# Decoder with 16-wide heads: interleaved head stacks, one transfer for a group's shift rows, and key stacks written by DMA

## The reference, cut to what matters

```python
# self-attention: q, k, v of LayerNorm(x), 512 keys
w = jnp.einsum('bshd,bzhd->bhsz', q, k) / jnp.sqrt(16.) / jnp.sqrt(16.)
w = jax.nn.softmax(w, axis=-1)
vw = jnp.einsum('bhsz,bzhd->bshd', w, v)
# cross-attention: q of LayerNorm(x), k and v of ctx_1024 (1024 keys), rotary q and k
scores = jnp.einsum('bhqd,bhkd->bhqk', q, k) * 16 ** -0.5
out = jnp.einsum('bhqk,bhkd->bhqd', jax.nn.softmax(scores, axis=-1), v)
```

## Time and profile before

| | us |
|---|---|
| median of 3 runs | 2225.75 |
| the profiled execution, its own time | 2233.84 |
| its span in the trace | 2232.0 |
| PE busy | 1995.9 (89%) |
| DVE busy | 1722.2 (77%) |
| ACT busy | 1347.4 (60%) |
| POOL busy | 262.1 (12%) |

### The profile page before, as it was taken

The page is one execution under the profiler, slowest core; times in us unless marked ns, Lnnn a source line. Parts: engine busy times, 40 slices in busy tenths (PEclk is TensorE's granted clock), DMA queues, the critical chain, the costliest instruction groups (busy, mean ns, idle before and its releaser), DMA issues.

```text
span 2232.0 us, 42943 instructions
## 1 busy us (share of the span) xinstructions
PE 1995.9 (89%) x17926; PEld 1125.7 (50%) x17926; DVE 1722.2 (77%) x2660; ACT 1347.4 (60%) x2001; POOL 262.1 (12%) x279
## 2 busy tenths in 40 slices
PE   2899988988989997989899998798998999889888
PEld 1576653423756764232466666333255667533335
DVE  7788878695878877779587887868767878786956
ACT  3566656587356654848536664675944666565782
POOL 2000001350000000135000000103400000011520
PEclk9999999999999999999999999999999999989999
DMA  6176730020046780001006776001001767400100
GB/s 262 36 125 120 126 69 1 1 92 14 20 77 121 124 135 20 2 19 78 11 20 107 125 125 119 1 2 76 21 10 41 121 118 123 93 1 1 76 2 10
DMA packets 417313, 147.66 MB, mean 66 GB/s; under 512 B 404440, under 2 KB 412768, under 8 KB 416224
## 3 DMA queue, kind: packets, MB, share of 16 engines
q1 hardware_dynamic: 416544, 142.82, 31.3%
q0 software_dynamic: 576, 2.10, 0.3%
HBM read 41.86 MB, written 2.10 MB: 20 GB/s over the span
## 4 chain that ended last, share of the span: by engine, by line
PE 57%; DVE 25%; DMA 7%; ACT 6%; issue 3%; SPq 0%; POOL 0%; POOLq 0%; DVEq 0%; ACTq 0%
PE ps L622 10%; DVE nmx L1940 10%; PE ps L624 10%; PE ps L623 10%; DMA arena<-arena 7%; PE ps L970 5%; PE ps L784 3%; PE ps L1037 3%; PE ps L956 3%; DVE arena L1752 3%; PE ps L924 2%; PE ps L779 2%; PE ps L778 2%; DVE st L1584 1%; PE ps L980 1%
## 5 line engine op out<-in xcount | busy, mean ns | idle before, releaser
L1940 DVE TENSOR_REDUCE nmx<-ps 128x2 f32<-128x1024 f32 x384 | 446.0, 1218 | 32.4 <-PE ps L924 30.5
L1449 ACT ACTIVATE arena<-ps 128x512 f32<-128x512 f32 x768 | 405.4, 603 | 55.8 <-PE ps L956 51.1
L622 PE MATMUL ps<-arena 128*128 128x512 f16 (+1 forms) x800 | 275.7, 345 | 1.1 <-DVE arena L1674 0.5
L623 PE MATMUL ps<-arena 128*128 128x512 f16 (+1 forms) x800 | 275.1, 344 | 0.0
L624 PE MATMUL ps<-arena 128*128 128x512 f16 (+1 forms) x800 | 274.4, 343 | 0.0
L1739 DVE TENSOR_SCALAR_CACHE_REDUCE ps<-ps 128x1536 f32<-128x1536 f32 x128 | 225.8, 1764 | 48.9 <-PE ps L624 48.3
L970 PE MATMUL ps<-arena 128*17 128x256 f32 x3072 | 238.7, 387 | 0.0
L1752 DVE SCALAR_TENSOR_TENSOR arena<-arena,rs 128x1536 f16<-128x1536 f32 x128 | 231.6, 1810 | 4.2 <-ACT arena L1343 4.2
L1343 ACT ACTIVATE arena<-arena,rs 128x1536 f16<-128x1536 f32 x128 | 200.8, 1568 | 40.1 <-DVE rs L1745 40.1
L1336 ACT ACTIVATE arena<-ps,nm 128x1536 f32<-128x1536 f32 x128 | 197.0, 1539 | 12.5 <-DVE ps L1739 12.5
L594 POOL TENSOR_TENSOR rstd<-ve,col 128x2 f32<-128x2 f32 x40 | 29.3, 732 | 1346.1 <-DVE ve L1845 907.1
(11 more groups left out here) (280 smaller groups left out, 3854.8 us busy)
## 6 DMA issues: line engine op xcount, KB each, us to landing
arena<-in_experts SPq DMA_DIRECT2D x4, 3840.0 KB, 11.5
arena<-in_weights SPq DMA_DIRECT2D x8, 929.0 KB, 12.7
arena<-in_ctx SPq DMA_DIRECT2D x4, 1024.0 KB, 5.8
arena<-arena SPq DMA_TRANSPOSE x256, 3.7
arena<-in_ctx_t SPq DMA_DIRECT2D x4, 1024.0 KB, 4.8
arena<-in_ternary SPq DMA_DIRECT2D x2, 1024.0 KB, 5.9
y<-in_x POOLq DMA_DIRECT2D x4, 512.0 KB, 4.3
x<-in_x SPq DMA_DIRECT2D x4, 512.0 KB, 3.7
```

Source lines behind the costliest of these rows:

```text
L622: mm(out_, lh, rh, start=(k == 0), stop=False)
L623: mm(out_, lh, rl_, start=False, stop=False)
L1449: A(pr_[:, n % RING, :], ps[:, 4 + n % 3, :], ACT.Exp).then_inc(b_exp.sem, 1)
L1940: V.tensor_reduce(nmx[:, g_ % 2, ch, :, pp, i], ps[:, 2 * (z % 2):2 * (z % 2) + 2, :], AX.X, ALU.max, negate=True)\
```

## The change

The rows of a head are interleaved: dim d takes rows 4d, 4d+1, 4d+2 (copies 0, 1, 2) and row 4d+3 is a pad, of which rows 3 and 35 of each head carry the shift (key side -64 and +64, `HC = 3`). So copy r of a pair's 32 rows of halves is a DMA with a partition stride of 4. Pairs 0 and 1 of the keys are still made on PE and ACT. Pairs 2 to 7 come by three DMAs each from `dk` (32 KB each in self-attention, 64 KB in cross-attention): 18 DMAs in each attention, 36 in a batch. The pads of pairs 2 to 7 are written by one DMA for each batch, from a table that is made at the start of the launch and stored in DRAM. The query stacks are made as before.

The shift rows of a group go out in one DMA (4 rows of 2 KB from 32 partitions); for that the maxima are laid out twice (`nm32`, 32 columns), which in self-attention is an added instruction on DVE for each group, and in cross-attention the minimum over both key halves that was there already, now 32 columns wide.

```diff
+                sp.dma_start(ks[HC:P:4, 2:8, :], pad_d.unsqueeze(1).to_broadcast([P // 4, 6, NCTX])).then_inc(pad_in.sem, 16)
+                def stack_keys(m_, p_):
+                    c, jj = divmod(p_, 4)
+                    n = (S, NCTX)[m_]
+                    for copy, part in enumerate((0, 0, 1)):
+                        sp.dma_start(ks[copy:P:4, p_, 0:n], dk[part][32 * jj:32 * jj + 32, c, 0:n]).then_inc(ks_in[p_].sem, 16)
                 def shift_rows(mode, g_):
                     sp.wait_ge(sl_free.sem, sl_free.at(b, mode.slot0 + mode.z_shift[g_] + 1))
-                    for e in range(2):
-                        for part in range(2):
-                            r0 = 64 * e + HR + part
-                            sp.dma_start(qs[r0:r0 + 1, 2 * g_:2 * g_ + 2, :], sh[8 * e:8 * e + 8, g_ % 2, part, :])\
-                              .then_inc(sh_in.sem, 16)
-                for g_ in range(GROUPS):
+                    sp.dma_start(qs[HC:P:32, 2 * g_:2 * g_ + 2, :], sh[0:32, g_ % 2, :]).then_inc(sh_in.sem, 16)
+                sp.wait_ge(lq_lo.sem, lq_lo.at(b, 1))
+                for p_ in range(2, 4):
+                    stack_keys(0, p_)
+                sp.wait_ge(lq_lo.sem, lq_lo.at(b, 3))
+                for p_ in range(4, 6):
+                    stack_keys(0, p_)
+                shift_rows(MODES[0], 0)
+                for p_ in range(6, 8):
+                    stack_keys(0, p_)
+                for g_ in range(1, GROUPS):
                     shift_rows(MODES[0], g_)
+                sp.wait_ge(kp_first_lo.sem, kp_first_lo.at(b, 1))
+                sp.wait_ge(kp_lo.sem, kp_lo.at(b, 1))
+                for p_ in range(2, 4):
+                    stack_keys(1, p_)
                 shift_rows(MODES[1], 0)
-                for done, n in ((lv_mm, 6), (k_st, LH), (q_st, LH)):
+                sp.wait_ge(kp_lo.sem, kp_lo.at(b, 3))
+                for p_ in range(4, 8):
+                    stack_keys(1, p_)
+                for done, n in ((lv_mm, 6), (k_st, 4), (q_st, LH)):
                     sp.wait_ge(done.sem, done.at(b, n))
+                for p_ in range(2, 8):
+                    sp.wait_ge(ks_in[p_].sem, ks_in[p_].at(b, 96))
...
@@ score_slot (PE)
-                    n = LH // 2 * mode.m + 2 * g_ + pp + 1
-                    pe.wait_ge(k_st.sem, k_st.at(b, n))
-                    pe.wait_ge(q_st.sem, q_st.at(b, n))
+                    p_ = 2 * g_ + pp
+                    if p_ < 2:
+                        pe.wait_ge(k_st.sem, k_st.at(b, 2 * mode.m + p_ + 1))
+                    else:
+                        pe.wait_ge(ks_in[p_].sem, ks_in[p_].at(b, 48 * (mode.m + 1)))
...
@@ between_cross (PE; between_self alike)
                 elif a in CROSS_SELECT:
-                    select_k(b, 1, CROSS_SELECT.index(a) + 1)
+                    if a == CROSS_SELECT[0]:
+                        select_k(b, 1, 1)
                     select_q(b, 1, CROSS_SELECT.index(a) + 1)
...
@@ max_slot (DVE)
-                if mode.nch == 2 and (a + 1) % mode.per_group == 0:
+                if (a + 1) % mode.per_group == 0:
                     dve.wait_ge(sl_free.sem, sl_free.at(b, mode.slot0 + z + 1))
...
+                    if mode.nch == 2:
+                        last = TT(nm32[:, g_ % 2], by_ch[0], by_ch[1], ALU.min)
+                    else:
+                        last = TS_(nm32[:, g_ % 2], by_ch[0], 1.0, None, ALU.mult)
+                    last.then_inc(nm_done.sem, 1)
...
@@ start of the launch (DVE)
+            own.mark(V.tensor_reduce(sh_lo[:], pad[:, 0, :, HC], AX.X, ALU.add))
+            own.link(V.tensor_reduce(k_pad[:], pad[:, 1, :, HC], AX.X, ALU.add))
+            own.link(TT(k_pad[:], k_pad[:], sh_lo[:], ALU.subtract))
             own.link(TS_(k_pad[:], k_pad[:], 64.0, None, ALU.mult))
+            TS_(ks[:, 4, :], ks[:, 4, :], k_pad[:], None, ALU.mult).then_inc(pad_made.sem, 1)
+            second = ident[:].rearrange("p (e n) -> p e n", n=16)[:, 0:2, 8:16]
+            own.link(V.tensor_reduce(sh_lo[:], second, AX.XY, ALU.add))
+            own.link(TS_(sh_lo[:], sh_lo[:], 1.0 / 64.0, None, ALU.mult))
```

More of the change, by code:

```diff
@@ L32 @@
 LH, LD = 16, 16
-HR = 48
-SR = HR + 2
+HC = 3
 GROUPS = 4
@@ L253, in decoder @@
         assert lay.at == 98304
-        sh = lay.take([2, 2, P], F16)
+        sh = lay.take([2, P], F16)
         lay = Layout()
@@ L264, in decoder @@
         assert lay.at <= 53760
+        pad_d = nc.dram_tensor("pad_d", (P // 4, NCTX), F16, kind="Internal").ap()
         ps = c_.enter_context(nc.psum_tensor("ps", [P, 8, 512], F32))
@@ L283, in decoder @@
         sel_set = sig("sel_set")
-        sel_mm, k_st, q_st = sig("sel_mm", 32), sig("k_st", LH), sig("q_st", LH)
+        sel_mm, k_st, q_st = sig("sel_mm", 20), sig("k_st", 4), sig("q_st", LH)
+        pad_in, pad_made, pad_out = sig("pad_in", 16), sig("pad_made"), sig("pad_out")
+        ks_in = [None, None] + [sig(f"ks_in{p_}", 2 * 48) for p_ in range(2, 8)]
         var_ready, rstd_ready = sig("var_ready", 10), sig("rstd_ready", 10)
@@ L1482, in stacked_q @@
             def stacked_q(b, m_, p_):
-                act.wait_ge(sel_mm.sem, sel_mm.at(b, LH * m_ + 2 * p_ + 2))
+                act.wait_ge(sel_mm.sem, sel_mm.at(b, 10 * m_ + (2 * p_ + 2 if p_ < 2 else p_ + 3)))
                 A(qs[:, p_, :], ps[:, 5 + m_, :], ACT.Copy, scale=(LD ** -0.5, 1.0)[m_]).then_inc(q_st.sem, 1)
@@ L1941, in max_slot @@
                     .then_inc(sl_free.sem, 1)
-                if mode.nch == 2 and (a + 1) % mode.per_group == 0:
+                if (a + 1) % mode.per_group == 0:
                     dve.wait_ge(sl_free.sem, sl_free.at(b, mode.slot0 + z + 1))
-                    both_ch = nmx[:, g_ % 2].rearrange("p k e c i -> p k (e c i)")
-                    TT(both_ch[:, 0], both_ch[:, 0], both_ch[:, 1], ALU.min).then_inc(nm_done.sem, 1)
+                    by_ch = [nmx[:, g_ % 2, k].rearrange("p e c i -> p e (c i)").unsqueeze(2).to_broadcast([P, 2, 2, 2 * NT])
+                             for k in range(mode.nch)]
+                    if mode.nch == 2:
[3 more added lines that the diff above has]
+                    last.then_inc(nm_done.sem, 1)
             def shift_split(b, mode, g_):
@@ L1950, in shift_split @@
                 if n >= 2:
-                    dve.wait_ge(sh_in.sem, sh_in.at(b, 64 * (n - 1)))
+                    dve.wait_ge(sh_in.sem, sh_in.at(b, 16 * (n - 1)))
                 dve.wait_ge(sl_mm.sem, sl_mm.at(b, 2 * (mode.mm0 + z + 1)))
-                src = ps[0:16, 2 * (z % 2), 0:P]
-                own.link(TS_(sh[0:16, g_ % 2, 0, :], src, 1.0 / 64.0, None, ALU.mult))
-                STT(sh[0:16, g_ % 2, 1, :], src, 1.0 / 64.0, sh[0:16, g_ % 2, 0, :], ALU.mult, ALU.subtract)\
-                    .then_inc(sl_free.sem, 1)
+                src, dst = ps[0:32, 2 * (z % 2), 0:P], sh[0:32, g_ % 2, :]
+                own.link(TS_(dst, src, 1.0 / 64.0, None, ALU.mult))
+                STT(dst, src, sh_lo[0:32], dst, ALU.mult, ALU.subtract).then_inc(sl_free.sem, 1)
             def slots(b, mode, a0, a1):
@@ L2137, in _ @@
             own.mark(TS_(taps[:], col[:, COL["cw"]:COL["cw"] + 3 * NM], mw[:, 0:1], None, ALU.mult))
-            pad = ident[:].rearrange("p (e n) -> p e n", e=2)[:, :, HR:SR]
-            own.link(V.tensor_reduce(k_pad[:], pad, AX.XY, ALU.add))
+            pad = ident[:].rearrange("p (e h n) -> p h e n", e=2, h=2)
+            own.mark(V.tensor_reduce(sh_lo[:], pad[:, 0, :, HC], AX.X, ALU.add))
+            own.link(V.tensor_reduce(k_pad[:], pad[:, 1, :, HC], AX.X, ALU.add))
+            own.link(TT(k_pad[:], k_pad[:], sh_lo[:], ALU.subtract))
             own.link(TS_(k_pad[:], k_pad[:], 64.0, None, ALU.mult))
+            TS_(ks[:, 4, :], ks[:, 4, :], k_pad[:], None, ALU.mult).then_inc(pad_made.sem, 1)
+            second = ident[:].rearrange("p (e n) -> p e n", n=16)[:, 0:2, 8:16]
+            own.link(V.tensor_reduce(sh_lo[:], second, AX.XY, ALU.add))
+            own.link(TS_(sh_lo[:], sh_lo[:], 1.0 / 64.0, None, ALU.mult))
             dve.wait_ge(b2_hi.sem, 1)
```

45 lines of the change are left out of this document (29 added, 16 removed).

## The result

The changed kernel takes 2174.91 us (median of 4 runs, 2171.07 to 2176.4), the kernel before in the same comparison 2224.35 (2221.53 to 2230.8): ratio 0.976, 95% interval 0.974 to 0.978. The forecast was 2208 us, with a range from 2197 to 2221, so it gained 49 us where 18 were expected. The profiled executions are 2233.84 us (span 2232.0) and 2171.07 us (span 2169.3).

The account below looks back on a forecast made before the run. The prediction took PE (57% of the chain) and DVE (25%) as the bound, DVE setting the pace in mid cross-attention. Its terms summed to -17.7 us, taking the median from 2225.75 to 2208 us, range 2197 to 2221.

Parts of the forecast that it names:

- The change part by part: The prediction's list of terms, summed against the profiled execution of 2233.84 us; the difference to the median was carried over.
- selects of keys, cross-attention: Cross-attention's opening: without the key selects DVE no longer idles behind six slots; 4.0 us a batch, 16.0 us saved.
- one transfer for a group: Shift rows of both attentions: one DMA instead of four lands them 1.9 us earlier; 5.5 us saved, between 3 and 6.5.
- the experts' load: Cross-attention: the load, issued behind 12 stack DMAs, may delay group 1's shift rows; 2.0 us lost, between 0 and 8.
- the minimum beside POOL: Cross-attention: POOL starts later, so a DVE minimum takes 0.18 instead of 0.85 us; 1.4 us saved, at most 2.7.
- self-attention, selects and added copy: Self-attention: fewer key selects save 2.0 us, an added DVE copy for each group loses 3.6 us.
- start of the launch: Launch start: PE waits for extra small DVE instructions and the pads' product; 1.6 us lost, between 1 and 2.5.
- Rival C: Attention openings: PE, now waiting for DVE, drops to half clock; +70 us, 2296 us; chance 0.02.
- case D: Whole launch: the sum holds with its terms at their good ends; -27.4 us, 2198 us; chance 0.11.

Follow-up runs that it names:

- E2: The changed kernel with 224 unused bytes per partition ahead of the arena, as misplaced as before: 2202.25 us, ratio 0.987 to the kernel before.
- E1: The kernel before with six small tensors moved behind the arena, which then starts on a multiple of 512: 2200.84 us, ratio 0.987.
- E4: The changed kernel with key stacks of pairs 2 to 7 again made by PE and ACT: 2194.71 us, ratio 0.984 to the kernel before.
- E8: The changed kernel with a group's shift rows again sent by four transfers instead of one: 2201.40 us, ratio 0.987 to the kernel before.
- E11: The changed kernel with every key-stack transfer followed by another of its size: 2214.29 us, ratio 0.994 to the kernel before.
- E9: The changed kernel with 224 unused bytes ahead of the arena, but the transposes' source alone on a multiple of 256: 2176.78 us, ratio 0.977.

## Why the prediction was wrong

**The failed step** is the silent one in "The change part by part": only the two attentions and the start of the launch have terms, so the latent, windowed, routed and ternary stages were held unchanged because their instructions were. `nm32` and `sh_lo` moved the arena by 288 bytes, from 224 past a multiple of 256 to 0, and the transposes' source with it. The term was put at nothing; it is worth about 24 us (E2 against the changed kernel, 0.987 against 0.976 of 2225 us) to 30 us (E1), and it made the range miss. The mechanism is not in the prediction at all. It could have been asked for: the diff shows two tensors ahead of the arena, and TensorE's longest DMA waits were on these transposes.

The terms beside what was measured, in us over the launch:

| term | forecast | measured |
|---|---|---|
| latent and all other stages | 0 | -24 to -30 |
| selects of keys, cross-attention | -16.0 | -17.0 (E4, less the minima) |
| one transfer for a group | -5.5 | -6.1 (E1 to E4) |
| the experts' load | +2.0 | 0 |
| the minimum beside POOL | -1.4 | -1.9 |
| self-attention, selects and added copy | +1.6 | -0.1 (E1) to -0.7, in a scatter of some 5 |
| start of the launch | +1.6 | +1.3 |

**Selects of keys, cross-attention: right.** The forecast was 4.0 us a batch, at most 4.3; E4 gives 4.25. The opening of batch 0 gave 4.5, with 0.20 us behind slot 10 that the prediction had not listed. The query selects behind slots 13 to 16, of which I expected up to 0.45 us, left no idle time.

**The minimum: right, cause included.** The forecast had read from the earlier trace rows that the 0.85 us go with a working POOL, and took 1.4 us off. All traces bear this out.

**One transfer for a group: right when alone, wrong as a term to be added.** With the key stacks in the same queue it is worth 26 us (E8). In a row: from E1 the stacks by DMA alone give nothing (2201.4 against 2200.8), one transfer alone 6, both together 25. The sum came out near because the two were made together; that they depend on each other the prediction did not see.

**The experts' load: no loss.** The forecast was 0.5 us a batch, and 1.5 us with the long issue, which was the true one (0.62 us). There is no wait for group 1's rows. In batch 0 the load goes out at 454.4 and has landed at 466.5 by its slower part, 11.7 us after that part's issue, where I took 12.8; the rows are needed at 467.2. It is narrow, as E11 shows.

**Self-attention: not resolved.** E4, with the selects back on PE, takes 245.9 us, the changed kernel 246.8, E1 246.9. Neither the 0.5 us a batch of the selects nor the 0.9 of the copy can be told from the scatter.

**The start:** the wait before the first products is 32.4 us, 31.1 before: +1.3 for 1.6.

**Rival C** appears, small. Windows of the changed kernel's self-attention, batch 0 (columns as above):
```profile
356.00:360.00 4.00, 3.47 (x23) 1.16 (x21) 3.97 (x4) 2.55 (x6) 0.00 (x0) 1.00 0.13 36
360.00:362.00 2.00, 1.14 (x6) 0.42 (x6) 1.97 (x4) 1.96 (x5) 0.00 (x0) 0.82 0.00 0
362.00:368.00 6.00, 6.00 (x38) 0.98 (x37) 4.34 (x6) 3.06 (x6) 0.00 (x0) 0.50 0.02 4
```
After PE's less busy stretch (1.14 of 2.00 us) the granted clock is 0.50, the 1.2 GHz level, for 6 us, and VectorE waits 0.7 us twice. That batch's self-attention takes 62.9 us, the quickest 60.8. The kernel before had such a batch too (63.6 us; over 1993 to 2000 us PE is busy for 5.78 us with a clock of 0.87, over 2000 to 2010 the clock is 0.75). So the prediction's sentence that no window of before with so little work has a lower clock was read from three windows and is wrong for the whole trace. In cross-attention's opening, where I had placed C, the clock stays at 1.00:
```profile
432.00:446.00 14.00, 11.81 (x71) 4.53 (x70) 13.93 (x16) 5.38 (x9) 6.96 (x7) 1.00 0.00 1
```
**With the address held,** the change is worth 28.7 us by E2 (20 to 37 by its interval), both kernels 224 past a multiple of 256, and some 23 to 26 us by E1 against the changed kernel, both on a multiple. That would be 2197 to 2202 us, inside the range at its low edge, and near case D (2198) or the forecast's own low end (2202). What is above the 17.7 forecast and has a place is cross-attention: -25.0 us from E1 to the changed kernel for -20.9 forecast. Half of this difference of 4.1 us is the loss of 2.0 us at the experts' load that did not come. The few us between the two estimates are within the noise; the profiled execution of before was itself 8 us over its median.

## What to carry to other kernels

A new tensor of a few bytes moves every later one: before pricing a diff, ask what lies behind it and which DMA reads it; a DMA transpose whose source starts off a multiple of 256 bytes lost 0.9 to 1.3% of this kernel. Small transfers on a shared queue can't be priced one by one: what stands ahead of them decides, and slack is counted to the landing of the large transfer ahead, not to its issue. Here neither the stacks by DMA nor the single transfer gave a third of what both gave. And a stage's gain can hold something else: a few VectorE instructions were short only because GpSimd had not begun yet.

## What the runs showed of the hardware

- A DMA transpose within the on-chip memory (128 rows of 1536 two-byte values) lands in a median of 3.2 to 3.3 us when its source starts 0 or 256 bytes past a multiple of 512, and in 3.7 to 3.8 us at 32, 128 or 224 past a multiple of 256. Its packets of 256 bytes take a mean of 20 ns in the one case and of 23 to 24 in the other. A destination 224 past a multiple plays no part that can be measured (E9).
- A plain transfer of 32 rows within the on-chip memory has an issue of 0.59 us and lands in 1.9 us (rows of 1 KB) or 2.1 us (2 KB), against 0.35 us of issue for the load of 3.8 MB.
- One small transfer issued 1.2 us after that load landed 10.8 us later; one issued 9.2 us after it was not waited for, though it was needed 3.6 us later.
- A minimum of two small tiles on VectorE (0.18 us) that starts during a TENSOR_TENSOR of GpSimd (1.15 us) ends 0.03 to 0.05 us after it, up to 1.19 us in all.
